# A layer of linear attention and a soft tree: keys' 128x128 transposes go from TensorE to a transposing DMA

## The chip, the cores and the metric

The kernel runs on one core of one Trainium2 chip. The metric is the device time in microseconds (us) of one execution. TensorE (PE) multiplies matrices into PSUM banks; VectorE (DVE), ScalarE (ACT) and GpSimd (POOL) work on SBUF, the first two on PSUM as well; SyncE (SP) issues DMAs. Each engine works through its own list in order and waits on semaphores.

## The reference

The input x is 4 batches of 2048 tokens of 256 features. With xn, its layer norm, the output is x + attention(xn) + tree(xn). Cut to what matters here:

```python
def _phi(x):
    return jax.nn.elu(x) + 1.0
Q = _phi((x @ Wq + bq).reshape(bs, n, H, D))        # H = 16 heads, D = 64
K = _phi((x @ Wk + bk).reshape(bs, n, H, D))
V = (x @ Wv + bv).reshape(bs, n, H, D)
def step(carry, qkv):                                # over the tokens
    KV, Ks = carry
    qi, ki, vi = qkv
    KV = KV + jnp.einsum('bhd,bhe->bhde', ki, vi)
    Ks = Ks + ki
    num = jnp.einsum('bhd,bhde->bhe', qi, KV)
    den = jnp.einsum('bhd,bhd->bh', qi, Ks)
    return ((KV, Ks), num / (den[..., None] + EPS))
...
return out @ Wo + bo
...
gate = jax.nn.sigmoid(q_flat @ routers.T)            # the tree, from the same xn
leaf_prob = _leaf_probs(gate)                        # 256 leaves, 8 levels
ret = leaf_prob @ leaf_values                        # then @ Wout_w.T + Wout_b
```

## The kernel before

The 8192 tokens are 16 blocks of 512, the 16 heads 8 pairs; a unit is one pair of heads in one block, so there are 128 units. Products with weights are made in three passes, high by high, high by low and low by high part. The scan is worked in chunks of 64 tokens: sums of outer products of keys and values are carried from chunk to chunk (`carry`, on DVE), and within a chunk masked scores do the rest.

For unit n each pass through PE's loop, called a stretch here, has two parts. First `tiled(n)`: 64x64 products for the output of unit n, the outer products of unit n+1, and the scores of unit n+1. Then the fills of `unit_fills`: each writes one of six PSUM banks, which another engine must drain before the next use. A fill is a head (transposes of xn or of leaf probabilities, six matmuls of V, or twelve of the gates) in bank W1, K in W0 and Q in S0 for unit n+2, a tail (six matmuls of V) in S1, `kT` in W0, and `oT`, the transposed output, in W1. The stretch of pair 7 also makes the block's output rows, `y`.

K is computed with features on partitions. ACT makes relu and exponential of it (`exponential`, L407 and L410), DVE adds and takes the maximum (`phi`, L520), which writes `kT`. The scores use `kT` so; the outer products need tokens on partitions. For that the fill `kT` transposes `kT` in four 128x128 fp32 transposes on PE (L702), and ACT copies the bank to `k_tok` (`copy_keys`, L420).

The order on each engine is written out by hand. ACT's per stretch is the copy of the scores (`copy_scores`, L434), then the fills' drains in their order. POOL masks the scores (`mask`, L329), adds the residual once a block (L337), and once a block works the tree's levels. SP, after the weights, loads a block of x (512 KB) and stores two halves of a block's output (256 KB each).

Of the kernel before, what the change touches and what calls it, by code (L numbers as in the profile page):

```python
# [8 lines left out]
F32R = mybir.dt.float32r  # L9

P = 128
# [15 lines left out]
def unit_fills(g, p, blocks):  # L27

    n = g * PAIRS + p
    ahead = divmod(n + 2, PAIRS) if n + 2 < blocks * PAIRS else None  # L30
    more = g + 1 < blocks
    head, tail = [], []
    if p == 0:
        head, tail = [("V1", 0, g)], [("V1", 1, g)]
    if p in (1, 2):
        tail = [("V1", p + 1, g)]
        if more:
            head = [("xT", p - 1, g + 1)]
    if p in (3, 4):
        head = [("leaf", p - 3, g)]  # L40
        if more:
            tail = [("V0", p - 3, g + 1)]
    if p in (5, 6) and more:
        head, tail = [("gate", p - 5, g + 1)], [("V0", p - 3, g + 1)]

    fills = [(name, W1) for name in head]
    if ahead:
        fills += [(("K", ahead[1], ahead[0]), W0), (("Q", ahead[1], ahead[0]), S0)]
    fills += [(name, S1) for name in tail]
    if p == PAIRS - 1:  # L50

        fills += [(("oT", p, g), W1), (("y", 0, g), O1)]
    if ahead:
        fills.append((("kT", ahead[1], ahead[0]), W0))
    fills.append((("y", 1, g), S1) if p == PAIRS - 1 else (("oT", p, g), W1))
    return fills
# [5 lines left out]
         (("kT", 1, 0), W0)]  # L62


def attention_and_tree_layer(nc, x, Wq, bq, Wk, bk, Wv, bv, Wo, bo,
# [45 lines left out]
    with ExitStack() as ctx:  # L111
# [37 lines left out]
        ex = sb("ex", [P, 2, TOK])  # L149
        k_tok = sb("k_tok", [P, CH, P])  # L150
        aT = sb("aT", [P, 2, 2, CH, D])
# [21 lines left out]
        for j, (name, weights, tiles, source) in enumerate((("wv", wv, KT_, Wv), ("wk", wk, KT_, Wk),  # L173
                                                            ("wq", wq, KT_, Wq), ("wo", wo, PAIRS, Wo))):
            for i, parts in enumerate(weight_halves(weights, stage[:, j], tiles, source)):
# [8 lines left out]
                     k_tok[:, :, :].rearrange("p c n -> p (c n)")]  # L184
# [41 lines left out]
        kv_filled = sem("kv_filled")  # L226
        sum_ready = sem("sum_ready")
# [28 lines left out]
        @block.sync  # L256
        def _(sp):
            sp.dma_start(x_in[:, 0], x_rows[0]).then_inc(x_loaded[0], 16)
            for i, b in enumerate((bq, bk)):
                sp.dma_start(bias_rows[i * PAIRS:(i + 1) * PAIRS, :],  # L260
                             b.rearrange("(r n) -> r n", n=P)).then_inc(loaded["bias"], 16)

            sp.wait_ge(consts_ready, 1)
            sp.dma_start(routers_in[:, 0], routers[0:P, :]).then_inc(loaded["small"], 16)
            sp.dma_start(routers_in[0:nodes - P, 1], routers[P:nodes, :]).then_inc(loaded["small"], 16)
            for dst, src in ((tree_wq_in, tree_Wq), (leaf_in, leaf_values), (wout_in, Wout_w)):
                sp.dma_start(dst, src.rearrange("(t p) n -> p t n", p=P)).then_inc(loaded["small"], 16)  # L267
# [16 lines left out]
            for g in range(BLOCKS):  # L284
                if g + 2 < BLOCKS:
                    sp.wait_ge(x_consumed, g + 1)
                    sp.dma_start(x_in[:, g % 2], x_rows[g + 2]).then_inc(x_loaded[g % 2], 16)
                for i in range(2):
                    name = ("y", i, g)
                    sp.wait_ge(drained[bank_of[name]], count_of[name])  # L290
                    sp.dma_start(out_rows[g, :, 2 * i:2 * i + 2, :],
                                 y_buf[:, 2 * i:2 * i + 2, :]).then_inc(y_stored, 16)
            sp.wait_ge(y_stored, 32 * BLOCKS)

        @block.gpsimd
        def _(pool):
# [68 lines left out]


# [3 lines left out]
            pool.wait_ge(leaf_step, 1)  # L370
            for n in range(UNITS):
# [4 lines left out]
                if n + 1 < UNITS:  # L376
                    mask(n + 1)
                if p == 1:
                    residual(g)
                    pool.wait_ge(x_consumed, g + 1)  # L380
# [11 lines left out]
        def _(act):  # L392
# [25 lines left out]
            def copy_keys(name):  # L418
                act.wait_ge(filled[bank_of[name]], count_of[name])
                act.activation(k_tok[:, :, :].rearrange("p c n -> p (c n)"), psum_of(name), ACT.Copy)\  # L420
                   .then_inc(drained[bank_of[name]], 1)

# [45 lines left out]
            copy_keys(("kT", 1, 0))  # L468

            for n in range(UNITS):  # L470
                if n + 1 < UNITS:
                    copy_scores(n + 1)
                for name, _ in unit_fills(n // PAIRS, n % PAIRS, BLOCKS):
# [5 lines left out]
                    elif kind == "kT":  # L479
                        copy_keys(name)  # L480
# [8 lines left out]
        def _(dve):  # L489
# [25 lines left out]
            def phi(name):  # L515
                kind, p, _ = name
                slot, dst = (0, kT) if kind == "K" else (1, qT)
                col = p + (PAIRS if kind == "K" else 0)
                dve.wait_ge(exp_ready, exp_count[name])
                dve.scalar_tensor_tensor(out=dst[:, p % 2], in0=psum_of(name), scalar=bias_one[:, col:col + 1],  # L520
# [94 lines left out]
            phi(("Q", 1, 0))  # L615

# [26 lines left out]
        def _(pe):  # L643
# [8 lines left out]
            def split_product(dst, lhs, rhs, tiles):  # L652
                steps = [s for t in range(tiles) for s in passes(lambda a, t=t: lhs(a, t), lambda a, t=t: rhs(a, t))]
                for i, (l, r) in enumerate(steps):
                    last = pe.matmul(dst, l, r, start=i == 0, stop=i == len(steps) - 1)  # L655
                return last
# [16 lines left out]
            def fill(name):  # L673
# [4 lines left out]
                if kind in "KQ":  # L678
                    wt = wk if kind == "K" else wq
                    last = split_product(dst, lambda a, t: wt[:, a, t, i * P:(i + 1) * P],  # L680
                                         lambda a, t: xnT[:, g % 2, a, t], KT_)
                elif kind in ("V0", "V1"):
                    half, n = int(kind[1]), 2 * HALF * D
                    last = split_product(dst, lambda a, t: xnT[:, g % 2, a, t, i * P:(i + 1) * P],
                                         lambda a, t: wv[:, a, t, half * n:(half + 1) * n], KT_)
# [14 lines left out]
                elif kind == "kT":  # L700
                    for c in range(CH):
                        last = pe.transpose(dst[:, c * P:(c + 1) * P], kT[:, i % 2, c * P:(c + 1) * P], ident[:, :])  # L702
                elif kind == "oT":
                    for c in range(CH):
                        if c == 1 and g * PAIRS + i + 1 < UNITS:
                            until(a_masked, 2 * (g * PAIRS + i) + 4)
# [169 lines left out]
            fill(("kT", 1, 0))  # L876
            until(split_lo_pool, len(LO_POOL))
            until(split_lo, len(LO_VECTOR))

            for n in range(UNITS):  # L880
# [3 lines left out]
                first_by_vector = fills[0][0][0] in ("V1", "xT", "leaf")  # L884
                for name, bank in fills:
# [43 lines left out]
```

## Time and profile before

| what | value |
|---|---|
| time, median of 3 runs | 1275.3 us (1274.66 to 1280.37) |
| profiled execution, time | 1273.15 us |
| profiled execution, span | 1271.4 us |
| granted clock of TensorE, mean | 0.997 |
| PE busy | 1244.6 us, 98% |
| DVE busy | 810.3 us, 64% |
| ACT busy | 622.4 us, 49% |
| POOL busy | 374.3 us, 29% |

The span is the time from the first to the last instruction in the profile. Busy shares say who has room, not who sets the end; that is read from the chain of waits.

### The profile page before, as it was taken

To read this page: it belongs to the slowest core of one execution; us is meant where nothing else is said; L and a number is where in the kernel's file an instruction comes from. 1 tells how busy PE (TensorE), PEld (TensorE's weight loads), DVE (VectorE), ACT (ScalarE), POOL (GpSimd) and SP (SyncE) were. 2 spreads that over 40 slices of the span, in tenths; PEclk is the share of its full clock that TensorE was granted. 3 is DMA by queue.
4 is the path that set the end of the run, shared out by engine and by line. 5 is a ranking of instruction groups with operands and counts; after the bars stand their busy time and mean duration, and the time that the engine had idled before them with its cause. 6 is when DMAs were issued, how large, how long until landed. Compare 5 with 4: busy or idle time off the path is not lost.

```text
span 1271.4 us, 48688 instructions
## 1 busy us (share of the span) xinstructions
PE 1244.6 (98%) x22173; PEld 1105.0 (87%) x22173; DVE 810.3 (64%) x2186; ACT 622.4 (49%) x1007; POOL 374.3 (29%) x590
## 2 busy tenths in 40 slices
PE   5899999999999999999999999999999999999997
PEld 5789888898988989889898988989889898898986
DVE  4675766757576574765757666575765758657473
ACT  4563654536446363653636445364553636536361
POOL 3424232132421413223142321324214132231320
PEclk9899999999999999999999999999999999999999
DMA  6000001000000000001000010000000000000000
GB/s 223 19 3 19 19 2 35 3 18 20 10 28 3 19 19 10 28 3 36 2 19 19 3 35 3 19 20 10 28 3 19 19 18 20 2 19 3 19 3 18
DMA packets 21597, 25.91 MB, mean 20 GB/s; under 512 B 1025, under 2 KB 19728, under 8 KB 21392
## 3 DMA queue, kind: packets, MB, share of 16 engines
q1 hardware_dynamic: 21392, 22.82, 5.5%
q8 instruction: 173, 2.83, 0.9%
q14 instruction: 32, 0.26, 0.1%
HBM read 14.43 MB, written 8.39 MB: 18 GB/s over the span
## 4 chain that ended last, share of the span: by engine, by line
PE 97%; DVE 1%; ACT 1%; DMA 1%; SPq 0%; issue 0%; DVEq 0%
PE s_pair L655 25%; PE w_pair L655 20%; PE o_pair L667 9%; PE s_pair L667 9%; PE o_pair L765 6%; PE kv_pair L740 5%; PE o_pair L779 5%; PE s_pair L729 5%; PE w_pair L709 4%; PE w_pair L702 4%; PE w_pair L689 3%; DMA ffn_tok<-in_L_ffn_Wout_w_dram 1%; DVE snaps L585 0%; SPq L267 0%; PE o_pair L655 0%; ACT ex L407 0%
## 5 line engine op out<-in xcount | busy, mean ns | idle before, releaser
L329 POOL TENSOR_SCALAR_AFFINE_SELECT aT<-aT 64x512 f32<-64x512 f32 x256 | 167.6, 655 | 833.0 <-ACT aT L434 824.7
L655 PE MATMUL w_pair<-xnT,wk 128*128 128x512 f32 x768 | 205.7, 403 | 0.7 <-ACT k_tok L420 0.7
L655 PE MATMUL s_pair<-xnT,wq 128*128 128x512 f32 x756 | 194.0, 392 | 0.0
L434 ACT ACTIVATE aT<-s_pair 128x512 f32<-128x512 f32 x128 | 76.4, 597 | 238.3 <-PE s_pair L729 238.3
L585 DVE TENSOR_TENSOR snaps<-kv_pair,snaps 128x65 f32<-128x65 f32 x768 | 173.3, 226 | 26.4
L520 DVE SCALAR_TENSOR_TENSOR kT<-w_pair,bias_one,ex 128x512 f32<-128x512 f32 x128 | 96.2, 751 | 122.7 <-ACT ex L410 122.6
L655 PEld LDWEIGHTS s_pair<-xnT,wq 128*128 128x128 f32 x756 | 142.1, 188 | 31.4
L655 PE MATMUL s_pair<-wv,xnT 128*128 128x512 f32 x648 | 168.7, 395 | 0.0
L410 ACT ACTIVATE ex<-ex 128x512 f32<-128x512 f32 x256 | 161.8, 632 | 8.1
L407 ACT ACTIVATE ex<-w_pair,neg_bias 128x512 f32<-128x512 f32 x130 | 89.5, 689 | 148.5 <-PE w_pair L655 148.5
L655 PEld LDWEIGHTS w_pair<-xnT,wk 128*128 128x128 f32 x768 | 136.1, 188 | 26.6 <-ACT k_tok L420 1.0
L655 PEld LDWEIGHTS s_pair<-wv,xnT 128*128 128x128 f32 x648 | 121.6, 188 | 28.6
L420 ACT ACTIVATE k_tok<-w_pair 128x512 f32<-128x512 f32 x128 | 76.4, 597 | 143.0 <-PE w_pair L702 143.0
L520 DVE SCALAR_TENSOR_TENSOR qT<-s_pair,bias_one,ex 128x512 f32<-128x512 f32 x126 | 94.3, 748 | 59.6 <-ACT ex L410 59.6
L765 PE MATMUL o_pair<-snaps,qT 64*64 64x65 f32 x3584 | 112.2, 225 | 3.5 <-DVE state L585 3.5
L544 DVE TENSOR_TENSOR oT<-w_pair,oT 128x512 fp32r<-128x512 f32 x128 | 88.3, 690 | 27.4 <-ACT oT L430 27.4
L667 PE MATMUL o_pair<-wo,oT 128*128 128x256 f32 x768 | 94.7, 279 | 0.0
L667 PE MATMUL s_pair<-wo,oT 128*128 128x256 f32 x768 | 94.7, 279 | 0.0
L667 PEld LDWEIGHTS o_pair<-wo,oT 128*128 128x128 f32 x768 | 91.9, 188 | 0.0
L667 PEld LDWEIGHTS s_pair<-wo,oT 128*128 128x128 f32 x768 | 91.9, 188 | 0.0
L562 DVE TENSOR_TENSOR o_tok<-o_pair,rden 128x512 f32<-128x512 f32 x128 | 88.5, 691 | 4.4
L765 PEld LDWEIGHTS o_pair<-snaps,qT 64*64 64x64 f32 x3584 | 83.6, 135 | 8.7 <-issue 8.4
(105 smaller groups left out, 1953.7 us busy)
## 6 DMA issues: line engine op xcount, KB each, us to landing
x_in<-in_L_attn_x_dram SPq DMA_DIRECT2D x16, 512.0 KB, 3.9
out_dram<-y_buf SPq DMA_DIRECT2D x32, 256.0 KB, 2.1
stage<-in_L_attn_Wv_dram SPq DMA_DIRECT2D x2, 512.0 KB, 8.0
stage<-in_L_attn_Wk_dram SPq DMA_DIRECT2D x2, 512.0 KB, 9.6
stage<-in_L_attn_Wq_dram SPq DMA_DIRECT2D x2, 512.0 KB, 10.8
stage<-in_L_attn_Wo_dram SPq DMA_DIRECT2D x2, 512.0 KB, 9.1
bv_all<-in_L_attn_bv_dram SPq DMA_DIRECT2D x1, 512.0 KB, 8.6
ffn_tok<-in_L_ffn_Wq_dram SPq DMA_DIRECT2D x1, 256.0 KB
```

The lines of the kernel that those rows point to most:

```text
L329: pool.affine_select(out=part, in_=part, compare_op=ALU.is_ge, fill=0.0, base=0, pattern=[[0, 2 * CH], [1, D]], channel_multiplier=-1).the ...
L407: act.activation(ex[:, slot], psum_of(name), ACT.Relu, scale=-1.0, bias=neg_bias[:, col:col + 1])\
L410: act.activation(ex[:, slot], ex[:, slot], ACT.Exp, scale=-1.0).then_inc(exp_ready, 1)
L420: act.activation(k_tok[:, :, :].rearrange("p c n -> p (c n)"), psum_of(name), ACT.Copy)\
L434: act.activation(aT[:, n % 2].rearrange("p h c q -> p h (c q)"), s_pair[:, :, 0:CH * D], ACT.Copy).then_inc(s_copied, 1)
L520: dve.scalar_tensor_tensor(out=dst[:, p % 2], in0=psum_of(name), scalar=bias_one[:, col:col + 1], in1=ex[:, slot], op0=ALU.add, op1=ALU.max)\
L544: dve.tensor_tensor(oT[:, 1, p], psum_of(name), oT[:, 0, p].bitcast(F32), ALU.subtract)\
L562: dve.tensor_tensor(o_tok[:, :, :, :].rearrange("p b t (h e) -> p b (t h) e", e=D), v[:, :, :, 0:D], rden[:, :, :].unsqueeze(3).to_broadca ...
L585: dve.tensor_tensor(dst, added, so_far, ALU.add).then_inc(sum_ready, 1)
L655: last = pe.matmul(dst, l, r, start=i == 0, stop=i == len(steps) - 1)
L667: last = pe.matmul(dst[:, (c % 2) * hid:(c % 2 + 1) * hid], oT[:, a, t, cols] if t < PAIRS else leafT[:, a, t - PAIRS, cols], wo[:, b, t] ...
L765: last = pe.matmul(output_at(t, h, a), qT[rows_of(h), p % 2, t * P + a * D:t * P + (a + 1) * D], before, start=turn == 0 and half not in b ...
```

## The change

- K is filled three units ahead instead of two, and first in each stretch, ahead of the head. K of unit 2 goes into the start.
- For all units from 2 on the fill `kT` on PE and its copy on ACT are gone. In their place POOL copies `kT`, seen as 16-bit halves, into two planes (`take_apart`, 1024 elements per partition); SP issues a transposing DMA of the planes (`turn_keys`, 128 x 1024 elements of 2 bytes, 256 KB); ACT interleaves the two halves into `k_tok` (`put_together`).
- ACT does `put_together(n+2)` right behind the copy of the scores of unit n+1, ahead of the exponentials of the keys of unit n+3. POOL does `take_apart(n+3)` behind `mask(n+1)`. There is one buffer each of planes, turned planes and `k_tok`.
- PE waits for the mask before the last matmul of Q, and for `k_tok` before the last matmul of the tail.
- On SP the loads and stores stand between the transposing DMAs: the two stores of a block behind the last transposing DMA of that block, the load behind the one of pair 2.

```diff
-    ahead = divmod(n + 2, PAIRS) if n + 2 < blocks * PAIRS else None
+    keys = divmod(n + 3, PAIRS) if n + 3 < blocks * PAIRS else None
+    queries = divmod(n + 2, PAIRS) if n + 2 < blocks * PAIRS else None
...
-    fills = [(name, W1) for name in head]
-    if ahead:
-        fills += [(("K", ahead[1], ahead[0]), W0), (("Q", ahead[1], ahead[0]), S0)]
+    fills = [(("K", keys[1], keys[0]), W0)] if keys else []
+    fills += [(name, W1) for name in head]
+    if queries:
+        fills.append((("Q", queries[1], queries[0]), S0))
     fills += [(name, S1) for name in tail]
+    fills.append((("oT", p, g), W1))
...
+            def turn_keys(m):
+                sp.wait_ge(k_apart, m - 1)
+                if m > 2:
+                    sp.wait_ge(k_whole, m - 2)
+                sp.dma_start_transpose(k_turned[:, :, :], k_planes[:, :, :].rearrange("p s t -> p (s t)"))\
+                  .then_inc(k_turned_in, 16)
...
+            def take_apart(m):
+                g, p = divmod(m, PAIRS)
+                pool.wait_ge(drained[bank_of["K", p, g]], count_of["K", p, g])
+                if m > 2:
+                    pool.wait_ge(k_turned_in, 16 * (m - 2))
+                pool.tensor_copy(k_planes[:, :, :], kT[:, m % 2].bitcast(U16).rearrange("p (t s) -> p s t", s=2))\
+                    .then_inc(k_apart, 1)
+                pool.wait_ge(k_apart, m - 1)
...
                 if n + 1 < UNITS:
                     mask(n + 1)
+                if n + 3 < UNITS:
+                    take_apart(n + 3)
...
+            def put_together(m):
+                act.wait_ge(k_turned_in, 16 * (m - 1))
+                act.wait_ge(kv_filled, m)
+                act.activation(k_tok[:, :, :].rearrange("p c f -> p (c f)").bitcast(U16)
+                               .rearrange("p (n s) -> p s n", s=2),
+                               k_turned[:, :, :].rearrange("p (s c) f -> p s (c f)", s=2), ACT.Copy).then_inc(k_whole, 1)
...
                 if n + 1 < UNITS:
                     copy_scores(n + 1)
+                if n + 2 < UNITS:
+                    put_together(n + 2)
...
-                until_drained(("kT", p, g))
+                if n < 2:
+                    until_drained(("kT", p, g))
+                else:
+                    until(k_whole, n - 1)
...
-                    if kind == "kT":
-                        until_drained(("K", i, g))
-                    fill(name)
+                    fill(name, masked if kind == "Q" else whole if bank == S1 and kind != "y" else None)
```

On PE, in the stretch of unit 1, the fills stood so before: transposes of xn, K (`xnT,wk`), Q (`xnT,wq`), V (`wv,xnT`), the keys' transposes (`ident,kT`) and the output's (`ident,o_tok`):

```order
L689 MATMUL w_pair<-ident,xn 128x128 [waits bank1_drained,xn_ready]
L689 MATMUL w_pair<-ident,xn 128x128 x3
L655 MATMUL w_pair<-xnT,wk 128x512 x6
L655 MATMUL s_pair<-xnT,wq 128x512 [waits s_copied]
L655 MATMUL s_pair<-xnT,wq 128x512 x5
L655 MATMUL s_pair<-wv,xnT 128x512 x6
L702 MATMUL w_pair<-ident,kT 128x128 [waits bank0_drained]
L702 MATMUL w_pair<-ident,kT 128x128 x3
L709 MATMUL w_pair<-ident,o_tok 128x128 [waits bank1_drained]
```

The same stretch after the change:

```order
L705 MATMUL w_pair<-xnT,wk 128x512 [waits bank0_drained]
L705 MATMUL w_pair<-xnT,wk 128x512 x5
L740 MATMUL w_pair<-ident,xn 128x128 [waits bank1_drained,xn_ready]
L740 MATMUL w_pair<-ident,xn 128x128 x3
L705 MATMUL s_pair<-xnT,wq 128x512 [waits s_copied]
L705 MATMUL s_pair<-xnT,wq 128x512 x4
L705 MATMUL s_pair<-xnT,wq 128x512 [waits a_masked]
L705 MATMUL s_pair<-wv,xnT 128x512 x5
L705 MATMUL s_pair<-wv,xnT 128x512 [waits k_whole]
L758 MATMUL w_pair<-ident,o_tok 128x128 [waits bank1_drained]
```

K has moved ahead of the head, the four keys' transposes are gone, and two waits stand before the last matmuls of Q and V.

On ACT, in the stretch of unit 3, from the copy of the scores (`aT<-s_pair`) to the copy of the output, before:

```order
L434 ACTIVATE aT<-s_pair 128x512 [waits s_filled]
L400 ACTIVATE leafT<-w_pair 128x512 [waits bank1_filled]
L407 ACTIVATE ex<-w_pair,neg_bias 128x512 [waits bank0_filled]
L410 ACTIVATE ex<-ex 128x512 [waits relu_ready]
L407 ACTIVATE ex<-s_pair,neg_bias 128x512 [waits bank2_filled]
L410 ACTIVATE ex<-ex 128x512 [waits relu_ready]
L420 ACTIVATE k_tok<-w_pair 128x512 [waits bank0_filled]
L430 ACTIVATE oT<-w_pair 128x512 [waits bank1_filled]
```

And after the change:

```order
L479 ACTIVATE aT<-s_pair 128x512 [waits s_filled]
L464 ACTIVATE k_tok<-k_turned 128x2x512 [waits kv_filled,k_turned_in]
L444 ACTIVATE ex<-w_pair,neg_bias 128x512 [waits bank0_filled]
L447 ACTIVATE ex<-ex 128x512 [waits relu_ready]
L437 ACTIVATE leafT<-w_pair 128x512 [waits bank1_filled]
L444 ACTIVATE ex<-s_pair,neg_bias 128x512 [waits bank2_filled]
L447 ACTIVATE ex<-ex 128x512 [waits relu_ready]
L475 ACTIVATE oT<-w_pair 128x512 [waits bank1_filled]
```

The write of `k_tok` went from the end of the stretch to the place behind the scores' copy and waits for the DMA (`k_turned_in`); the head's copy now stands behind the keys' exponential.

On SP, from the last loads of the start to the first block's stores, after the change (before, only loads and stores stood there):

```order
L279 DMA stage<-in_L_attn_Wo_dram 128x4x256 x2
L296 DMA_TRANSPOSE k_turned<-k_planes 128x8x128 [waits k_apart]
L296 DMA_TRANSPOSE k_turned<-k_planes 128x8x128 [waits k_whole,k_apart] x3
L315 DMA x_in<-in_L_attn_x_dram 128x4x256 [waits x_consumed]
L296 DMA_TRANSPOSE k_turned<-k_planes 128x8x128 [waits k_whole,k_apart] x5
L303 DMA out_dram<-y_buf 128x2x256 [waits bank5_drained]
L303 DMA out_dram<-y_buf 128x2x256 [waits bank3_drained]
```

Each transposing DMA waits for POOL's planes and for ACT's use of the one before; a load or a store comes behind it in the queue.

## Rows read from the trace of the kernel before

**Rows 1.** The page: busy time by engine, and the chain that ended last, by engine.

```profile
PE 1244.6 (98%) x22173; PEld 1105.0 (87%) x22173; DVE 810.3 (64%) x2186; ACT 622.4 (49%) x1007; POOL 374.3 (29%) x590
...
PE 97%; DVE 1%; ACT 1%; DMA 1%; SPq 0%; issue 0%; DVEq 0%
```

**Rows 2.** Windows: stretches of pairs 3, 6, 7 and 0 (start:end; length, busy times).

```profile
610.44:618.17 7.73, 7.73 (x165) 6.67 (x158) 5.85 (x16) 4.92 (x9) 1.31 (x2) 1.00 0.02 4
...
634.69:643.39 8.70, 8.70 (x172) 7.65 (x167) 5.26 (x15) 4.92 (x9) 1.31 (x2) 1.00 0.01 2
643.39:663.21 19.82, 19.82 (x271) 19.06 (x265) 7.86 (x25) 4.33 (x8) 11.06 (x21) 1.00 0.06 19
663.21:671.95 8.74, 8.74 (x162) 7.41 (x156) 7.36 (x21) 4.31 (x8) 1.32 (x2) 1.00 0.08 26
```

**Rows 3.** Timeline of the stretch of pair 3: start, duration, engine, line.

```profile
610.12 0.60 ACT L434 ACTIVATE aT<-s_pair 128x512 f32<-128x512 f32 x1 [1.03 <-PE s_pair L729]
...
610.45 0.66 PE L689 MATMUL w_pair<-ident,ffn_tok 128*128 128x128 f32 x4
...
610.86 1.63 PE L655 MATMUL w_pair<-xnT,wk 128*128 128x512 f32 x6
611.14 0.60 ACT L400 ACTIVATE leafT<-w_pair 128x512 fp32r<-128x512 f32 x1 [0.43 <-PE w_pair L689]
...
612.33 1.53 PE L655 MATMUL s_pair<-xnT,wq 128*128 128x512 f32 x6
...
612.53 0.69 ACT L407 ACTIVATE ex<-w_pair,neg_bias 128x512 f32<-128x512 f32 x1 [0.79 <-PE w_pair L655]
613.25 0.63 ACT L410 ACTIVATE ex<-ex 128x512 f32<-128x512 f32 x1
...
613.70 1.56 PE L655 MATMUL s_pair<-wv,xnT 128*128 128x512 f32 x6
...
613.91 0.75 DVE L520 SCALAR_TENSOR_TENSOR kT<-w_pair,bias_one,ex 128x512 f32<-128x512 f32 x1 [0.77 <-ACT ex L410]
...
615.10 0.60 PE L702 MATMUL w_pair<-ident,kT 128*128 128x128 f32 x4
615.29 0.75 DVE L520 SCALAR_TENSOR_TENSOR qT<-s_pair,bias_one,ex 128x512 f32<-128x512 f32 x1 [0.62 <-ACT ex L410]
...
615.53 0.60 PE L709 MATMUL w_pair<-ident,o_tok 128*128 128x128 f32 x4
...
615.95 0.68 DVE L529 TENSOR_TENSOR v_aug<-s_pair,bv_all 128x512 f32<-128x512 f32 x1
...
616.06 0.27 PE L765 MATMUL o_pair<-state,qT 64*64 64x65 f32 x1
...
617.13 0.65 PE L729 MATMUL s_pair<-qT,kT 64*64 64x64 f32 x32
...
618.18 0.66 PE L689 MATMUL w_pair<-ident,ffn_tok 128*128 128x128 f32 x4
```

**Rows 4.** Timeline of pair 7's stretch, where K already stands first.

```profile
643.39 1.66 PE L655 MATMUL w_pair<-xnT,wk 128*128 128x512 f32 x6
...
645.09 0.69 ACT L407 ACTIVATE ex<-w_pair,neg_bias 128x512 f32<-128x512 f32 x1 [1.43 <-PE w_pair L655]
```

**Rows 5.** Groups by line and form on ACT and POOL: operations of 128x1024 elements.

```profile
L396 ACT ACTIVATE wo<-stage 128x1024 fp32r<-128x1024 f32 x2 | 2.1, 1058 | 0.0
```

```profile
L337 POOL TENSOR_TENSOR y_buf<-x_in,y_bias 128x1024 f32<-128x1024 f32 x16 | 38.7, 2419 | 1.3
...
L345 POOL TENSOR_SCALAR ffn_tok<-ffn_tok 128x1024 f32<-128x1024 f32 x16 | 17.6, 1102 | 1.4
```

**Rows 6.** DMA issues: count, KB each, median us from issue to landing.

```profile
x_in<-in_L_attn_x_dram SPq DMA_DIRECT2D x16, 512.0 KB, 3.9
out_dram<-y_buf SPq DMA_DIRECT2D x32, 256.0 KB, 2.1
stage<-in_L_attn_Wv_dram SPq DMA_DIRECT2D x2, 512.0 KB, 8.0
```

More of the change, by code:

```diff
@@ L9 @@
 F32R = mybir.dt.float32r
+U16 = mybir.dt.uint16
 P = 128
@@ L44, in unit_fills @@
         head, tail = [("gate", p - 5, g + 1)], [("V0", p - 3, g + 1)]
-    fills = [(name, W1) for name in head]
-    if ahead:
-        fills += [(("K", ahead[1], ahead[0]), W0), (("Q", ahead[1], ahead[0]), S0)]
+    fills = [(("K", keys[1], keys[0]), W0)] if keys else []
+    fills += [(name, W1) for name in head]
+    if queries:
+        fills.append((("Q", queries[1], queries[0]), S0))
     fills += [(name, S1) for name in tail]
+    fills.append((("oT", p, g), W1))
     if p == PAIRS - 1:
[L52 to L55, printed above, removed]
+        fills += [(("y", 0, g), O1), (("y", 1, g), S1)]
     return fills
@@ L226, in attention_and_tree_layer @@
         kv_filled = sem("kv_filled")
+        k_apart = sem("k_apart")
+        k_turned_in = sem("k_turned_in")
+        k_whole = sem("k_whole")
         sum_ready = sem("sum_ready")
@@ L282, in _, with store @@
             load("wo1")
[L284 to L287, printed above, removed]
+            def turn_keys(m):
[4 more added lines that the diff above has]
+                  .then_inc(k_turned_in, 16)
+            def store(g):
                 for i in range(2):
@@ L292, in _ @@
                                  y_buf[:, 2 * i:2 * i + 2, :]).then_inc(y_stored, 16)
+            turn_keys(2)
+            for n in range(UNITS):
+                g, p = divmod(n, PAIRS)
+                if p == 0 and g:
+                    store(g - 1)
+                if n + 3 < UNITS:
+                    turn_keys(n + 3)
+                if p == 2 and g + 2 < BLOCKS:
+                    sp.wait_ge(x_consumed, g + 1)
+                    sp.dma_start(x_in[:, g % 2], x_rows[g + 2]).then_inc(x_loaded[g % 2], 16)
+            store(BLOCKS - 1)
             sp.wait_ge(y_stored, 32 * BLOCKS)
@@ L468, in _ @@
             copy_keys(("kT", 1, 0))
+            exponential(("K", 2, 0))
             for n in range(UNITS):
@@ L671, in output_rows, with fill @@
                 return last
-            def fill(name):
+            def fill(name, at_last=None):
                 kind, i, g = name
@@ L701, in fill @@
                     for c in range(CH):
-                        last = pe.transpose(dst[:, c * P:(c + 1) * P], kT[:, i % 2, c * P:(c + 1) * P], ident[:, :])
+                        last = pe.transpose(dst[:, c * P:(c + 1) * P], kT[:, i, c * P:(c + 1) * P], ident[:, :])
                 elif kind == "oT":
                     for c in range(CH):
-                        if c == 1 and g * PAIRS + i + 1 < UNITS:
-                            until(a_masked, 2 * (g * PAIRS + i) + 4)
                         to = dst[:, c * P:(c + 1) * P].rearrange("p (a q) -> p a q", a=2)
@@ L876, in _ @@
             fill(("kT", 1, 0))
+            fill(("K", 2, 0))
             until(split_lo_pool, len(LO_POOL))
@@ L882, in _, with masked, whole @@
                 fills = unit_fills(n // PAIRS, n % PAIRS, BLOCKS)
-                first_by_vector = fills[0][0][0] in ("V1", "xT", "leaf")
+                first_by_vector = any(bank == W1 and name[0] in ("V1", "xT", "leaf") for name, bank in fills)
+                def masked():
+                    if n + 1 < UNITS:
+                        until(a_masked, 2 * n + 4)
+                def whole():
+                    if n + 2 < UNITS:
+                        until(k_whole, n + 1)
                 for name, bank in fills:
@@ L900, in _ @@
                             until_drained(("leaf", t, g))
-                    if kind == "kT":
-                        until_drained(("K", i, g))
-                    fill(name)
+                    fill(name, masked if kind == "Q" else whole if bank == S1 and kind != "y" else None)
+                    if kind == "y" and i == 0:
+                        whole()
+                masked()
+                whole()
 _INS = ['L0_attn_x', 'L0_attn_Wq', 'L0_attn_bq', 'L0_attn_Wk', 'L0_attn_bk', 'L0_attn_Wv', 'L0_attn_bv',
```

27 lines of the change are left out of this document (16 added, 11 removed).

## The prediction

> **What bounds the kernel now.** I read the chain of waits first: 97% of it lies on PE, and PE is busy 98% of the span [rows 1]. Nothing but PE's own list sets the end, so work taken off PE is worth its time, as long as no other engine comes to be waited for. The windows by stretch say what period the others must keep: 7.73 us in the four short stretches of a block (pairs 1 to 4), 8.7 in pairs 5, 6 and 0, and 19.82 in pair 7, which makes the output rows; in each PE is busy for its whole length [rows 2]. DVE has 5.85 and ACT 4.92 busy us of the 7.73: room, but what counts is the order in which they get to it. Then I read one short stretch in order of time [rows 3].
>
> **What goes off PE.** The keys' transposes start at 615.10 and the output's at 615.53 [rows 3]: 0.43 us of PE's list, and nothing beside them. 126 of the 128 such fills go: 126 x 0.43 = 54 us at most. K and the head only change places. PE's floor for a short stretch is then 7.73 - 0.43 = 7.30.
>
> **What the rest then does in a short stretch.** I take the stretch's first fill as time 0, and spacings from [rows 3]. PE: K at 0, head at 1.47 (612.33 - 610.86), Q at 1.88 (head 0.41), V at 3.25, output's transposes at 4.65 (V 1.40), tiled part at 5.18 (0.53), scores at 6.25 (617.13 - 616.06 = 1.07 into it), next stretch at 7.30. ACT: the copy of the scores ends at 0.27 (610.72 - 610.45). Interleaving writes 1024 elements per partition; the nearest row is ACT's 128x1024 copy, 1.06 us [rows 5] (below, 0.60 as for 512 elements; nothing in the trace is above): it ends at 1.33, if the DMA has landed. K is ready for ACT 1.70 after its start (645.09 - 643.39, where K already stands first [rows 4]). So the interleave fits the gap of 0.37 ahead of K's relu and costs nothing by itself. Then relu 0.69 and exponential 0.63 with gaps of 0.03: 1.70 to 3.05; the head's copy 0.60, which stood ahead of K before, to 3.68; Q's pair to 5.06. DVE then makes qT, 5.10 to 5.85, and the values of V, 0.68, to 6.53 [rows 3]. The scores of the second head need V's bank drained: 6.53 + 0.05 against 6.25. So PE waits 0.3, and the stretch takes 7.6: of 0.43 only 0.13 are left in pairs 1, 3 and 4. In pair 2 DVE takes V ahead of Q, qT ends at about 6.33, and 0.3 is left. With the gates' longer head (pairs 5 and 6, scores at 7.3, values at 7.4) 0.32 is left, in pair 0, where the normalising of the next block stands ahead on DVE, 0.25, and in pair 7, whose end is the output rows, all of 0.43. Sum per block: 3 x 0.13 + 0.3 + 2 x 0.32 + 0.25 + 0.43 = 2.0 us. Fifteen blocks give 30; for the last, which has no heads for a next block and so shorter stretches, I count nothing. At the start ACT waits for the first transposing DMA with little ahead of it; I charge 3 us once. That is 27 us off.
>
> **The new ring.** The interleave stands ahead of the next keys' exponentials, and these lead to the next interleave. Once round: interleave 1.06, relu and exponential 1.38 with gaps, 0.04 to DVE, its kT 0.75, 0.06, POOL's copy, 0.05, the DMA from issue to landing, D, and 0.04 back to ACT. POOL's copy of 1024 elements per partition: 1.10 as the one-input 128x1024 row; above, 2.42 as the two-input one [rows 5]; it has one input, so I take 1.10. The ring is 4.48 + D, and it must go round once a stretch: in 7.6, so D up to 3.1 is free. The masks of POOL, 1.31 busy a stretch [rows 2], are over by 1.8, long before kT at 3.8; behind the copy stand the residual (2.42, pair 1) and the levels (pair 7), which end within their stretches. On SP the load of x (3.9 us) and the stores (2.1) come behind a transposing DMA and have landed before the next is issued, a period of 7.6 later [rows 6].
>
> D is in no row. Nothing in the trace turns a matrix by DMA. Below, the same 256 KB as a plain store lands in 2.1; above, 512 KB of x in 3.9; the weights at the start, queued behind each other, in 8.0 [rows 6]. It can't be below the plain transfer by anything that I see. I take the middle of 2.1 and 3.9, D = 3.0, since it moves the same bytes in smaller pieces: the ring is 7.48 and stays hidden.
>
> Beside these rows stands a rule that speaks against the change. The Trainium skill, "VectorE: DVE Perf Modes", section on the three transpose paths, gives 1309 ns for one 128x128 block of 2-byte elements by the DMA's crossbar; eight of them one after another would be an estimated 10.5 us, and no run here shows it. By that the ring would be 15 us and the kernel far slower; the same skill's "Advanced Engine Details and Errata", X-Bar Transpose, calls such DMAs as fast as regular ones, and by that the forecast holds.
>
> **The rivals.**
> (a) Slower: the transposing DMA is late and the ring sets the stretch. What decides is D: each 0.1 us above 3.1 puts 0.1 on each of four short stretches, less the 0.4 of gap ahead of K's relu once a block. At D = 3.9, the row of twice the bytes, the ring is 8.38: 4 x 0.78 - 0.4 = 2.7 per block, 41 us on top of the forecast. At 4.5 pairs 5 and 6 are caught as well (floor 8.43): 4 x 1.38 + 2 x 0.55 - 0.4 = 6.2, 93 us. Beyond, every us of D costs 6 x 15 = 90. The gain of 27 is eaten (1.8 per block) at a ring of 8.15, D = 3.7. A POOL copy of 2.42 in place of 1.10 shifts this by 1.3. For it: 2-byte pieces, and turned in small blocks; against it: the DMA engines are idle, with a share of 0.01 to 0.08 in these stretches [rows 2]. Times: 1279 to 1300 for D near 3.8 to 4, 1341 at 4.5, more above.
> (b) The whole 0.43 comes off: ACT reads Q and V in time, as DVE would have to slip 0.3 less than I make it. For it: my step from qT to the scores leans on a margin of some tenths. Time 1275 - 54 = 1221.
> (c) The two cancel, D at 3.6 to 3.8: within 0.5%, 1269 to 1281. That is also the answer if the transposes cost PE less than 0.43, against which the spacing of 0.43 in each stretch speaks [rows 3].
>
> **How the numbers follow.** The profiled execution took 1273.15 us beside a span of 1271.4, with 1275.3 as the median: 1273 - 27 = 1246, put on the median 1248. Half a per cent, 6.4 us, is about what a measurement of this kernel can tell from no change. Chances: the forecast (D to 3.5, 1240 to 1265) 0.45; (b) 0.08; (c) 0.08; (a) 0.39, of which 0.13 lies above 1340. Faster 0.53, same 0.08, slower 0.39. With cases of both signs, the range of eight in ten runs from 1222, just over (b), to 1340, where (a) has D = 4.5; the likeliest case alone has 1240 to 1265.
>
> **What would show it.** Right: short stretches of 7.4 to 7.6; the DMA view with some 3 us from issue to landing; ACT's interleave starting with the end of the copy of the scores, or idle before it for under 0.4; PE idle some 0.3 before the scores, ended by DVE's values. Wrong by (a): ACT idle ahead of the interleave, ended by the DMA, and PE idle ahead of V's last matmul, ended by the interleave, or ahead of the output's transposes, ended by the head's drain. Wrong by (b): 7.3 and no idle time of PE. POOL's copy well off 1.1, or ACT's well off 1.06, shifts all of it.

## The result and the profile after

The changed kernel takes 1287.7 us (median of 6 runs, 1281.93 to 1288.58), the kernel before 1277.15 (6 runs, 1274.66 to 1280.37). The ratio is 1.0074, with an interval of 1.0049 to 1.0099: slower by 0.7%. The forecast was 1248, faster. The profiled execution took 1288.58 us beside a span of 1286.9, at a mean granted clock of 0.992 (0.997 before).

The page after, busy times and the chain by engine, to set beside [rows 1]:

```profile
PE 1217.8 (95%) x21669; PEld 1054.8 (82%) x21669; DVE 798.4 (62%) x2186; ACT 698.7 (54%) x1007; POOL 505.2 (39%) x716
...
PE 51%; DMA 19%; ACT 11%; issue 8%; POOL 5%; DVE 5%; SPq 0%; POOLq 0%; DVEq 0%
...
L396 POOL COPY k_planes<-kT 128x1024 uint16<-128x1024 uint16 x126 | 131.2, 1041 | 362.8 <-issue 199.3
...
L464 ACT ACTIVATE k_tok<-k_turned 128x1024 uint16<-128x1024 uint16 x126 | 172.9, 1372 | 103.5 <-DMA k_turned<-k_planes 102.9
...
x_in<-in_L_attn_x_dram SPq DMA_DIRECT2D x16, 512.0 KB, 5.0
out_dram<-y_buf SPq DMA_DIRECT2D x32, 256.0 KB, 2.2
k_turned<-k_planes SPq DMA_TRANSPOSE x126, 3.1
```

PE is busy for 27 us less, but only half of the chain still lies on it, where 97% did. The rest runs through the DMA, ACT's interleave, DVE and POOL's copy: the new ring, which has become the bound. The two copies answer to [rows 5]: 1.04 us where 1.10 was taken, and 1.37 where 1.06 was. The DMA's median of 3.1 is close to the D of 3.0 that was taken. The median is not the whole of it; the view of the tile `k_turned` (durations in ns, waits in us and times):

```profile
L296 SPq DMA_TRANSPOSE k_turned<-k_planes x126: 1232/1232/2499, 45.4 to 1252.9; - x126
L464 ACT ACTIVATE k_tok<-k_turned x126: 1357/1372/1392, 48.7 to 1256.0; 128x1024 uint16<-128x1024 uint16 x126
...
  DMA k_turned<-k_planes: 102.9, 77
...
DMA to landing us min/median/max: 3.1/3.1/5.0
```

The time from issue to landing reaches 5.0, and ACT stood idle for it in 77 of 126 stretches. Windows on a stretch of pair 1 and on the next of pair 3, from one copy of the scores to the next (start:end; length, busy time of PE, PEld, DVE, ACT and POOL, granted clock, DMA share, GB/s):

```profile
602.88:610.26 7.38, 7.38 (x170) 6.26 (x162) 5.75 (x16) 5.60 (x8) 4.30 (x4) 1.00 0.13 25
617.73:628.30 10.57, 8.58 (x162) 7.15 (x158) 6.19 (x17) 5.41 (x9) 2.35 (x3) 0.88 0.39 90
```

The first is even shorter than the 7.6 of the forecast: 7.38 against 7.73 in [rows 2], and PE without a gap. The second is the longest in the trace; PE has stood idle for 2 us in it. The timeline of the second, beside [rows 3]:

```profile
617.73 0.60 ACT L479 ACTIVATE aT<-s_pair 128x512 f32<-128x512 f32 x1 [1.04 <-PE s_pair L778]
...
620.94 1.37 ACT L464 ACTIVATE k_tok<-k_turned 128x1024 uint16<-128x1024 uint16 x1 [2.62 <-DMA k_turned<-k_planes]
...
622.18 0.66 ACT L444 ACTIVATE ex<-w_pair,neg_bias 128x512 f32<-128x512 f32 x1
622.87 0.63 ACT L447 ACTIVATE ex<-ex 128x512 f32<-128x512 f32 x1
623.40 0.58 ACT L437 ACTIVATE leafT<-w_pair 128x512 fp32r<-128x512 f32 x1
623.53 0.75 DVE L567 SCALAR_TENSOR_TENSOR kT<-w_pair,bias_one,ex 128x512 f32<-128x512 f32 x1 [3.34 <-ACT ex L447]
...
624.20 0.68 DVE L559 TENSOR_TENSOR leafT<-w_pair,leafT 128x512 fp32r<-128x512 f32 x1
624.40 1.04 POOL L396 COPY k_planes<-kT 128x1024 uint16<-128x1024 uint16 x1 [4.57 <-DVE kT L567]
...
624.93 0.66 PE L758 MATMUL w_pair<-ident,o_tok 128*128 128x128 f32 x4 [1.99 <-DVE leafT L559]
...
627.16 1.09 PE L778 MATMUL s_pair<-qT,kT 64*64 64x64 f32 x32
```

ACT had copied the scores by 618.33 and then waited 2.62 for the DMA. Everything queued behind the interleave on ACT moved with it: the keys' exponentials, then the head's copy. DVE's part of the head came 1.99 late for PE, whose transposes of the output need the head's bank. And `kT` was late as well, so POOL's copy and the next DMA start late: the delay is handed to the next stretch.

Part of the 10.57 is the clock. Behind this idle time of PE the granted clock fell to its lower level (1.2 GHz; 0.50 of full speed) for 3.4 us:

```profile
625.70:629.10 3.40, 3.40 (x129) 3.28 (x125) 2.86 (x9) 1.12 (x2) 0.07 (x1) 0.50 0.43 82
```

PE's scores took 1.09 there and 0.65 in [rows 3]. It happened once more in blocks 1 to 14, at 390.2, in a stretch of 10.50, also behind an idle time of PE (1.81). PE is busy for 8.58 and 8.68 in these two stretches and for some 7.7 in the other late ones of pair 3: about 1 us each, 2 us of the loss. The other late stretches of these blocks ran at the full clock, and experiment 2 has no such fall in them and takes the same time.

Worked from the starts of the copies of the scores in the trace, blocks 1 to 14, in us:

| stretch of pair | 0 | 1 | 2 | 3 | 4 | 5 | 6 | 7 | block |
|---|---|---|---|---|---|---|---|---|---|
| before, mean | 8.78 | 7.74 | 7.74 | 7.73 | 7.74 | 8.77 | 8.71 | 19.83 | 77.03 |
| after, mean | 8.33 | 7.54 | 8.15 | 8.92 | 8.23 | 8.81 | 8.41 | 19.37 | 77.75 |
| after, shortest | 8.33 | 7.38 | 7.47 | 7.83 | 7.63 | 8.31 | 8.40 | 19.35 | |
| after, longest | 8.34 | 8.87 | 9.13 | 10.57 | 9.22 | 9.43 | 8.42 | 19.39 | |
| after, interleave on POOL (below) | 8.33 | 7.38 | 7.47 | 7.37 | 7.39 | 8.36 | 8.40 | 19.38 | 74.09 |

Pairs 7, 0 and 6 gain what they should and hardly vary; the loss sits in pairs 2 to 5 and varies from block to block, though the program does the same in each block. Of the 15.5 us that the span grew by, 10 lie in these fourteen blocks (14 x 0.72), 3.6 in the first block (its first stretch 12.29 against 10.24), the rest at the two ends.

Why some DMAs are late shows in the DMA view, whose first row is the busy share of the 16 DMA engines in 40 slices (a packet counts in the slice in which it starts). A transfer that landed in 3.1, window 645.2 to 646.8:

```profile
DMA  0035799999999999999999999999999999432009
```

One that landed in 4.8, window 635.8 to 639.0:

```profile
DMA  0499999999990000000000000100000009999990
...
q1 hardware_dynamic: 1056, 0.26, 115.0%
q8 instruction: 1, 0.02, 3.4%
q14 instruction: 1, 0.01, 0.6%
...
k_turned<-k_planes SPq DMA_TRANSPOSE x1, 4.8
```

The late transfer starts as usual, then for some 1.7 us hardly a packet starts, and then it ends. Inside it lies one packet of queue q8, 16 KB of instructions (the one of q14 comes at the end, behind the stop). The packets of the trace show the order: the q8 packet lasts from 635.96 to 637.70; 20 packets of the transfer that start between 636.40 and 636.71 stay open until 638.45 to 638.49; from 637.68 on, with the q8 packet done, 24 others run one after the other, and only then the 20 end and the rest follows.

Counted over all packets of the trace: the data of a transposing transfer take 1.4 us; 31 of the 126 take 1.8 to 3.1, and each of these 31 has a q8 packet in it; of the 95 others 35 touch one, at an edge. An edge can be enough: of the 29 landings over 4.0 us, 9 have their data through in under 1.8 and a q8 packet at the end, ahead of the landing. In all, 43 of the 126 landings come later than 3.3 us, and each of the 43 has a q8 packet between its first packet and its landing. The pages count these packets; the first line is of the kernel before, the second of the changed one:

```profile
q8 instruction: 173, 2.83, 0.9%
```

```profile
q8 instruction: 169, 2.77, 0.9%
```

Divided by TensorE's matmuls and weight loads (2 x 22173 and 2 x 21669), that is 64 bytes each in both, one packet per 256 of them. So these are taken for fetches of TensorE's list, and experiment 5 tests it. The kernel before had no transfer in these stretches to disturb but loads and stores.

### The profile page after: what moved, and what is told of

The parts are those of the page before. It is cut to its first block, busy times and chain, and to the rows that moved or that the text cites. A ratio compares the mean times of both kernels' runs of the same rounds, so it can differ in the third digit from the quotient of the medians.

```text
span 1286.9 us, 48282 instructions
## 1 busy us (share of the span) xinstructions
PE 1217.8 (95%) x21669; PEld 1054.8 (82%) x21669; DVE 798.4 (62%) x2186; ACT 698.7 (54%) x1007; POOL 505.2 (39%) x716
## 4 chain that ended last, share of the span: by engine, by line
PE 51%; DMA 19%; ACT 11%; issue 8%; POOL 5%; DVE 5%; SPq 0%; POOLq 0%; DVEq 0%
DMA k_turned<-k_planes 18%; PE w_pair L705 11%; PE s_pair L705 9%; PE o_pair L717 9%; PE s_pair L717 9%; ACT k_tok L464 6%; POOL k_planes L396 5%; PE o_pair L814 3%; ACT ex L447 3%; PE s_pair L778 2%; PE o_pair L828 2%; PE kv_pair L789 2%; PE w_pair L758 2%; ACT ex L444 2%; DVE kT L567 2%
## 5 line engine op out<-in xcount | busy, mean ns | idle before, releaser
L396 POOL COPY k_planes<-kT 128x1024 uint16<-128x1024 uint16 x126 | 131.2, 1041 | 362.8 <-issue 199.3
L464 ACT ACTIVATE k_tok<-k_turned 128x1024 uint16<-128x1024 uint16 x126 | 172.9, 1372 | 103.5 <-DMA k_turned<-k_planes 102.9
L705 PE MATMUL w_pair<-xnT,wk 128*128 128x512 f32 x768 | 212.0, 411 | 2.2 <-ACT k_tok L457 2.2
L705 PE MATMUL s_pair<-xnT,wq 128*128 128x512 f32 x756 | 200.7, 400 | 1.4 <-POOL aT L353 1.1
L705 PEld LDWEIGHTS s_pair<-xnT,wq 128*128 128x128 f32 x756 | 135.1, 188 | 27.0 <-POOL aT L353 2.2
L758 PE MATMUL w_pair<-ident,o_tok 128*128 128x128 f32 x512 | 81.2, 282 | 43.3 <-DVE leafT L559 27.3
L758 PEld LDWEIGHTS w_pair<-ident,o_tok 128*128 128x128 f32 x512 | 60.2, 142 | 75.1 <-DVE leafT L559 40.5
L444 ACT ACTIVATE ex<-s_pair,neg_bias 128x512 f32<-128x512 f32 x126 | 86.3, 685 | 34.0 <-PE s_pair L705 33.7
L475 ACT ACTIVATE oT<-w_pair 128x512 fp32r<-128x512 f32 x128 | 76.1, 595 | 52.6 <-PE w_pair L758 52.6
L778 PE MATMUL s_pair<-qT,kT 64*64 64x64 f32 x4096 | 98.9, 223 | 4.5 <-DVE qT L567 2.4
```

The costliest lines, as they stand in the source:

```text
L396: pool.tensor_copy(k_planes[:, :, :], kT[:, m % 2].bitcast(U16).rearrange("p (t s) -> p s t", s=2))\
L444: act.activation(ex[:, slot], psum_of(name), ACT.Relu, scale=-1.0, bias=neg_bias[:, col:col + 1])\
L464: act.activation(k_tok[:, :, :].rearrange("p c f -> p (c f)").bitcast(U16) .rearrange("p (n s) -> p s n", s=2), k_turned[:, :, :].rearrang ...
L758: last = pe.transpose(to[:, ::-1] if c % 2 else to, o_tok[:, c % 2, c // 2], ident[:, :])
L778: last = pe.matmul(s_pair[rows_of(a), h, t * D:(t + 1) * D], kT[rows_of(h), p % 2, at], qT[rows_of(h), p % 2, at], start=True, stop=True)
```

## The experiments

Why do pairs 2 to 5 lose what the other pairs gain? The expectations name the theories by letters. O: the new order of fills costs it. C: the load of x, behind pair 2's transposing DMA, collides. G: any transfer in this place is late, turning or not. F: TensorE's instruction fetches make a landing late, and the ring hands that on; against it S: the late places are fixed by the schedule. R: the ring through ACT's interleave is too long to catch up; against it L: a late landing costs the same whatever the ring. P: POOL's or ACT's traffic in SBUF slows DVE.

**1. The interleave on POOL.** The same copy, the same waits; ACT keeps its old work alone, so that a late DMA delays no exponential.

```diff
+            def put_together(m):
+                pool.wait_ge(k_turned_in, 16 * (m - 1))
+                pool.wait_ge(kv_filled, m)
+                pool.tensor_copy(k_tok[:, :, :].rearrange("p c f -> p (c f)").bitcast(U16)
+                                 .rearrange("p (n s) -> p s n", s=2),
+                                 k_turned[:, :, :].rearrange("p (s c) f -> p s (c f)", s=2)).then_inc(k_whole, 1)
...
                     mask(n + 1)
+                if n + 2 < UNITS:
+                    put_together(n + 2)
                 if n + 3 < UNITS:
                     take_apart(n + 3)
...
                     copy_scores(n + 1)
-                if n + 2 < UNITS:
-                    put_together(n + 2)
...
```

> The interleave goes from ScalarE to GpSimd, between the mask and the taking apart; all else as in the changed kernel. Theory F (the transposing DMA lands 3.1 us after its issue, but 4.4 to 5.0 us when one of TensorE's instruction fetches of 16 KB falls into it, and ScalarE's ring of 7.7 us has no room for that): the ring on GpSimd is 1.04 + 0.1 + 3.1 to 5.0 + about 1.04 = 5.3 to 7.2 us and has no exponentials in it, so late landings are hidden; short stretches 7.3 to 7.5 us, hardly an idle time of TensorE ended by the keys, time 1235 to 1245 us. Rival O (the loss is in the order of the fills, keys ahead of the head): no better than 1275 us. Rival P (GpSimd's or ScalarE's SBUF traffic slows VectorE): VectorE's operations longer than before, time over 1260 us.

1233.05 us (4 runs, 1230.73 to 1234.72), ratio 0.9651 (0.961 to 0.9692), 2 us below the expected range. Page and tile view:

```profile
PE 1201.2 (98%) x21669; PEld 1052.6 (85%) x21669; DVE 809.5 (66%) x2186; ACT 551.6 (45%) x881; POOL 675.7 (55%) x842
...
PE 95%; DMA 1%; POOL 1%; DVE 1%; ACT 1%; issue 1%; SPq 0%; POOLq 0%; DVEq 0%
```

```profile
L405 POOL COPY k_tok<-k_turned x126: 1332/1362/1374, 48.6 to 1200.5; 128x1024 uint16<-128x1024 uint16 x126
...
DMA to landing us min/median/max: 3.1/3.1/5.0
```

The DMA is as late as ever (29 of 126 transfers over 1.8 us, 32 landings over 4.0), but PE does not wait for it: the chain is back on PE, and short stretches with a late landing take the same 7.37 to 7.48 as the others. P falls as well: DVE is busy for 809.5 us, 810.3 before. The whole loss of 55 us against this kernel came from where the interleave stood, and 43 us of the transposes' 54 do come off (busy PE 1244.6 to 1201.2, time 1275.8 to 1233.05). In the stretch itself (timeline):

```profile
596.58 1.37 POOL L353 TENSOR_SCALAR_AFFINE_SELECT aT<-aT 64x512 f32<-64x512 f32 x2 [2.83 <-ACT aT L480]
598.60 1.36 POOL L405 COPY k_tok<-k_turned 128x1024 uint16<-128x1024 uint16 x1 [0.65 <-POOL aT L353]
600.08 1.04 POOL L396 COPY k_planes<-kT 128x1024 uint16<-128x1024 uint16 x1
```

**2. The load of x behind pair 6's transposing DMA instead of pair 2's.**

```diff
-                if p == 2 and g + 2 < BLOCKS:
+                if p == 6 and g + 2 < BLOCKS:
```

> The changed kernel with SyncE's load of x (512 KB) issued behind the transposing DMA of pair 6 in place of pair 2. Rival C (the load, issued 1.3 us behind the transposing DMA of pair 2, makes it late): the late landings go from the middle of the block to its end, where the long stretch hides them; 15 blocks x some 1.5 us, 1263 to 1270 us. Theory F: the load explains little, since landings of 4.4 us and more are as common in pairs 1, 3 and 4 as in pair 2; 1280 to 1290 us, within 0.5% of the changed kernel.

1286.5 us (6 runs), ratio 1.0073 (1.0048 to 1.0098); stretches 8.11, 8.58, 8.32 in pairs 2 to 4, where the changed kernel has 8.15, 8.92, 8.23. C falls. Of the 27 late units (counted as in experiment 5) 25 are late in the changed kernel too.

**3. Keys first alone.** The kernel before with K ahead of the head, its transposes on PE as they were.

```diff
-    fills = [(name, W1) for name in head]
+    fills = [(("K", ahead[1], ahead[0]), W0)] if ahead else []
+    fills += [(name, W1) for name in head]
...
```

> The kernel before with one part of the change alone: keys ahead of the head in each stretch; transposes stay on TensorE, keys two units ahead. By my hand sum ScalarE gets to the queries' exponential 0.6 us later, and VectorE is done with V 6.5 us into a stretch; with the transposes still on TensorE the scores start at 6.7 us, so nothing waits: 1272 to 1280 us, same as before. Rival O (this order is what costs): 1290 us or more, and idle time of TensorE ahead of the scores.

1276.96 us (10 runs), ratio 1.0011 (0.9986 to 1.0037). O falls: the order of fills by itself costs nothing that can be told from noise. That holds with the transposes still on PE; without them it may cost some 5 us (experiments 1 and 8, ratios of 0.9651 and 0.961, whose intervals overlap).

**4. A plain copy of the same 256 KB in place of the transposing DMA.**

```diff
-                sp.dma_start_transpose(k_turned[:, :, :], k_planes[:, :, :].rearrange("p s t -> p (s t)"))\
+                sp.dma_start(k_turned[:, :, :].rearrange("p c f -> p (c f)"), k_planes[:, :, :].rearrange("p s t -> p (s t)"))\
```

> The changed kernel with a plain DMA of the same 256 KB from the planes to the turned planes in place of the transposing one: nothing is turned, so this part of the computation is left out. It tells what is the transposing DMA's own. Theory F with lockstep (a fetch on one of the 16 DMA queues stops a transposing DMA on all of them): the plain copy lands in about 2.1 us as the 256 KB store does, and with a fetch in at most 3.2; the ring is 6.7 to 7.8 us and mostly hidden, 1235 to 1250 us. Rival G (any DMA here is as late, through the SBUF side or the semaphores): landings again up to 4.5 to 5 us in a third of the cases, over 1265 us.

1237.43 us (4 runs), ratio 0.9685 (0.965 to 0.9721). Page and tile view:

```profile
L464 ACT ACTIVATE k_tok<-k_turned 128x1024 uint16<-128x1024 uint16 x126 | 172.5, 1369 | 19.9 <-DMA k_turned<-k_planes 19.5
```

```profile
L296 SPq DMA_DIRECT2D k_turned<-k_planes x126: 464/465/532, 48.3 to 1203.0; - x126
...
DMA to landing us min/median/max: 2.3/2.3/4.6
```

The ring is 0.8 shorter and ACT's wait falls from 102.9 to 19.5 us. That no landing would pass 3.2 was wrong: 16 do, and three of them take 4.3 to 4.6. G falls, since it is far from a third that take so long, but the plain copy is not immune. Its transfer takes 0.83 us; 25 of 126 touch a fetch, and 18 of these take 1.35 to 2.98, while none of the other 101 passes 1.15. With 0.83 in place of 1.4 in transfer and 0.8 less to landing, it meets fewer fetches and the ring has room for most of them. The plain copy also moves in 128 packets of 2 KB, the transposing one in 1024 of 256 bytes; no run tells whether the turning or the packets make the difference.

**5. Forty more transposes at the start**, which shift TensorE's list against its blocks of 16 KB and change nothing else.

```diff
+            for _ in range(40):
+                pe.transpose(kv_pair[:, 0, 0:P], ident[:, :], ident[:, :])
```

> The changed kernel with 40 more 128x128 transposes of the identity on TensorE at the start, while it waits for the first loads; nobody reads them. They shift the places at which TensorE's 16 KB instruction fetches fall by 80 instructions and change nothing in the stretches. In the changed kernel 29 of the transposing DMAs reach ScalarE over 4.2 us after GpSimd's copy; with the load of x moved it was the same unit in 24 of 27. Theory F (the fetches make them late): the late units are others, at most 14 of the 29 late again, and about as many, 18 to 40 in all; time 1275 to 1295 us. Rival S (what stands in those stretches makes them late): at least 20 of the same 29.

1286.79 us (6 runs), ratio 1.0063 (1.0042 to 1.0083). Counting from the end of POOL's copy to the interleave, over 4.2 us is late, without the 15 units whose interleave stands behind the long stretch of pair 7: 29 units in the changed kernel, 28 here, and only 10 are the same (a recount makes those of experiment 2 25, not 24). By the landing alone, over 4.0 us, it is 29 and 29 with the same 10, and each of the 29 here has a q8 packet ahead of it too. With the fetches the late units move, in the same schedule: F is shown, S falls.

**6. ACT interleaves half the elements.**

```diff
-                               .rearrange("p (n s) -> p s n", s=2),
-                               k_turned[:, :, :].rearrange("p (s c) f -> p s (c f)", s=2), ACT.Copy).then_inc(k_whole, 1)
+                               .rearrange("p (n s) -> p s n", s=2)[:, :, 0:TOK // 2],
+                               k_turned[:, :, :].rearrange("p (s c) f -> p s (c f)", s=2)[:, :, 0:TOK // 2],
+                               ACT.Copy).then_inc(k_whole, 1)
```

> The changed kernel with ScalarE interleaving half of the elements (the other half of k_tok keeps what stood there, so half of the keys' part is left out). The interleave goes from 1.37 us to about 0.75 and the ring from 7.66 to about 7.05 us, below the 7.4 us of a short stretch without waits. Theory R (late landings cost what they do because the ring has no room, so that one late landing is handed from stretch to stretch): stretches recover after one late landing, 1245 to 1262 us. Rival L (each late landing costs its 1.7 us whatever the ring): 1278 us or more.

1254.49 us (4 runs), ratio 0.9818 (0.9796 to 0.984). The group on ACT:

```profile
L464 ACT ACTIVATE k_tok<-k_turned 128x512 uint16<-128x512 uint16 x126 | 99.3, 788 | 97.8 <-DMA k_turned<-k_planes 97.5
```

0.58 less per interleave takes 33 us off, though ACT waits for the DMA almost as long as before (97.5). The wait is the same, but the ring now has room: the stretch of a late landing still takes some 8.2 to 8.8, and the next one with a landing on time is back at 7.37 to 7.41 (pairs 3 and 4), where in the changed kernel it takes 7.6 to 7.9. R is shown, L falls. So the length of the interleave and the late landings cost what they cost together.

**7. ACT's interleave behind the keys' exponentials**, with a late DMA then delaying no exponential of K.

```diff
-                if n + 2 < UNITS:
-                    put_together(n + 2)
...
+                        if kind == "K":
+                            put_together(n + 2)
...
```

> The changed kernel with ScalarE's interleave behind the keys' relu and exponential, so that a late landing no longer holds the next keys: the ring is cut, and everything behind it on ScalarE is later by 1.37 us. By my hand sum the head's copy ends at 5.1 us into a stretch, VectorE drains its bank at 5.8, and the output's transposes wait from 4.65 on, then the scores: short stretches of 8.3 to 8.9 us, 1295 to 1325 us. If the ring were all that costs (theory R without the queue on ScalarE), 1235 to 1250 us.

1309.29 us (4 runs), ratio 1.0242 (1.0221 to 1.0263). Timeline of a short stretch:

```profile
608.87 1.36 ACT L464 ACTIVATE k_tok<-k_turned 128x1024 uint16<-128x1024 uint16 x1
...
610.11 0.56 ACT L437 ACTIVATE xnT<-w_pair 128x512 fp32r<-128x512 f32 x1
...
610.70 0.69 DVE L560 TENSOR_TENSOR xnT<-w_pair,xnT 128x512 fp32r<-128x512 f32 x1 [0.94 <-ACT xnT L437]
...
611.44 0.66 PE L759 MATMUL w_pair<-ident,o_tok 128*128 128x128 f32 x4 [0.63 <-DVE xnT L560]
```

Hardly a wait for the DMA is left (1.2 us in all), and it is slower still: ACT's 1.36 now stands ahead of the head's and of Q's drains in every stretch (8.15 us in pair 2, 8.5 in pairs 1, 3 and 4, hardly varying) instead of in the late ones. Neither of the two places that were tried for the 1.37 us in ACT's list between the scores and Q is a good one.

**8. The interleave on POOL as in experiment 1, and the head ahead of K again.** The part that differs from experiment 1:

```diff
-    fills = [(("K", keys[1], keys[0]), W0)] if keys else []
-    fills += [(name, W1) for name in head]
+    fills = [(name, W1) for name in head]
+    if keys:
+        fills.append((("K", keys[1], keys[0]), W0))
```

> The interleave on GpSimd and the head ahead of the keys again, as in the kernel before. Keys reach GpSimd's copy 0.4 us later, the DMA lands by 3.1 us into the next stretch when late, the interleave ends by 4.5, where TensorE wants it at 4.6; ScalarE is back to its old order, and VectorE's wait ahead of the scores goes. Short stretches 7.3 us in place of 7.38: 1226 to 1236 us. If the late landings no longer fit: over 1240 us, with TensorE idle before the last matmul of V, ended by the interleave.

1227.25 us (4 runs, 1226.75 to 1231.28), ratio 0.961 (0.9588 to 0.9632), the fastest here. Its page:

```profile
PE 1196.7 (98%) x21669; PEld 1050.5 (86%) x21669; DVE 809.3 (66%) x2186; ACT 559.0 (46%) x881; POOL 673.9 (55%) x842
```

The DMA, from the tile view:

```profile
DMA to landing us min/median/max: 3.1/3.4/4.9
```

Short stretches take 7.31 to 7.42 in the mean, against a floor of 7.30, though 59 of the 126 landings take over 4.0 us here, twice as many as in the changed kernel.

## Why the prediction was wrong

- **What goes off PE: right.** 0.43 per stretch and 54 at most; experiment 1 brought 43, experiment 8 50. That the changed kernel shows only 27 less of busy PE, with the same instructions as experiment 1, doesn't speak against it: short waits count as busy. The stretches of pair 4 that the ring holds to 7.63 to 7.71 show PE busy for their whole length, 0.3 more than on time; the longer ones of pairs 3 and 4 show some 7.7 as well; and two ran 3.4 us at clock 0.50.
- **The stretch without the ring: right in kind, too cautious.** The wait of the scores for V's bank was put at 0.3; on time it is about 0.08 (7.38 against 7.30). Stretches of 7.6 were expected in pairs 1, 3 and 4; 7.38 came in pair 1, and with the interleave on POOL in all three. The 2.0 us a block are 2.9 in experiment 1 (77.03 - 74.09).
- **Interleave 1.06: mis-sized.** It takes 1.37. On time it still fits ahead of K's relu, with 0.16 of ACT's idle time left in the stretch of pair 1 above:

```profile
604.92 0.69 ACT L444 ACTIVATE ex<-w_pair,neg_bias 128x512 f32<-128x512 f32 x1 [0.16 <-PE w_pair L705]
```

But the ring is 4.48 + 0.31 - 0.06 (POOL's 1.04) + 3.1 = 7.8 by the prediction's terms. Rings with an on-time landing that ACT has no idle time in but for the DMA take 7.63 to 7.9 in the trace, half of them up to 7.68. That is above the 7.38 that PE asks: in a row of short stretches not even an on-time landing is free, and a delay can't be made up. At most 4 x 0.3 a block come from that alone, an estimate of 18 us in fifteen blocks; on top of experiment 1's 1233 that is 1251, near the forecast of 1248. So this term and the one before nearly cancel, which is luck, and the miss is the next step's.
- **"D = 3.0" and "the DMA engines are idle": the step that failed.** The median of 3.1 is right, by luck, since 3.0 was the middle between two rows that turn nothing, and the ring was rightly named, with D as what decides it. But D was taken as one number. The share of 0.01 to 0.08 [rows 2] was read as "nothing there to meet", when the page of before already listed 173 instruction packets of 16 KB (above). A third of the landings (43 of 126) come later than 3.3, and 29 of them 1.2 to 1.9 later than the median. Experiments 1, 4, 5 and 6 together show it: move the fetches and the late units move; put a plain copy in its place and the transfer mostly escapes them; free the ring of ACT or shorten it and the same late landings cost nothing, or much less.
- **Rivals.** The mechanism is (a)'s, down to the signs named for it: ACT idle until the DMA, PE idle before the output's transposes until the head's drain. Its form is another: not a constant D above 3.7, but 3.1 with late ones. The time, 1287.7, lies within the 1279 to 1300 that (a) gave for a D near 3.8 to 4, and outside (c). (b)'s 1221 needed a free ACT; experiment 8 comes within 6 us of it.
- **The Trainium skill**, "VectorE: DVE Perf Modes", has 1309 ns for one block: the prediction's estimate of eight such blocks one after another, 10.5 us, is not borne out, since all eight are transferred in 1.4 us. "Advanced Engine Details and Errata", X-Bar Transpose, calls such DMAs as fast as regular ones: 3.1 against 2.3 us to landing, 1.4 against 0.83 in transfer, 1.23 against 0.46 for the issue on SP. That page is nearer, but the two are not equal here.

The changed kernel's time is experiment 1's plus 55 us: the ring that binds even with an on-time landing, and late landings that it can't absorb. How the 55 divide is not additive: with the DMA's 0.8 off the ring (and most late landings with it) 4 us are left of it, with 0.58 off the interleave 21.

## What to carry to other kernels

A new loop of several engines that must go round once a stretch needs room for its slowest transfer, not for its median; count what else the DMA engines carry, instruction fetches included. Put the step that waits for a DMA on an engine whose later work nobody waits for soon: the same copy of nearly 1.4 us cost 55 us on ACT and next to nothing on POOL. A moved copy may not be priced by its element count alone: here 1024 elements of 2 bytes, written at a stride of two, took 1.37 where 1024 of 4 bytes, written without gaps, took 1.06.

## What the runs showed of the hardware that was not expected

- A 16 KB instruction fetch that falls into an SBUF-to-SBUF transfer holds up the whole transfer, not one engine's share of it, often for over a microsecond: from 1.4 to at most 3.1 us with the turning, from 0.83 to at most 2.98 without. The Trainium skill, "Runtime: NRT & Kernel Launch", Instruction fetch mechanics, has the blocks of 16 KB and calls their cost mostly hidden; the size agrees with the 169 packets here. In the trace of before the cost is hidden from TensorE (173 packets, and no idle time of PE over 0.3 us that the profile leaves without a cause), but it is not hidden from a transfer. Why the other packets of the transfer wait for the held ones stays open.
- 16-bit halves interleaved at a stride of two, 128x1024: 1.37 us on ACT and 1.36 on POOL, where a 128x1024 fp32 copy takes 1.06 on ACT [rows 5]; taking apart, 1.04 on POOL. No run separates the size of the elements from the stride.
- Near the end of experiment 1 PE sits idle with nothing that the profile shows to wait for, here the two longest (timeline):

```profile
1189.17 0.45 PE L826 MATMUL o_pair<-v_aug,aT 64*64 64x65 f32 x13 [1.51 <-issue]
...
1198.04 0.27 PE L776 MATMUL s_pair<-qT,kT 64*64 64x64 f32 x1 [1.77 <-issue]
```

One stretch of the last block takes 10.94 there. Both begin while a q8 packet (1186.90 to 1187.78, 1195.71 to 1196.64) and a transposing transfer (until 1189.13 and 1197.93) overlap. Experiment 7 has two of the same length, 1.51 and 1.77, also with such an overlap, and no other trace of this case has one over 0.3. A fetch that comes late for TensorE itself would look like this; that the lengths repeat where the transfers end otherwise speaks against a delay handed on one to one. It was not tried and stays open.
